# New job orders for a two-layer decoder kernel, and its four weight-folding jobs moved five periods ahead

## The reference

```python
x = x + _L0_attn_ref(_layernorm(x), ...)    # 16 heads of 16, softmax
x = x + _L0_xattn_ref(_layernorm(x), ctx)   # 16 heads, 120 context rows, softmax
x = x + _L0_ffn_ref(_layernorm(x), ...)     # 256x256 weight quantised to int4, plus rank 16
x = x + _L1_attn_ref(_layernorm(x), ...)    # rotary positions, sigmoid instead of softmax
x = x + _L1_xattn_ref(_layernorm(x), ctx)   # one head of 256, softmax
x = x + _L1_ffn_ref(_layernorm(x), ...)     # two of 64 experts per 128 tokens
```

## Time and profile before

| | us |
|---|---|
| median of 3 runs (lowest, highest) | 1092.66 (1091.53, 1095.04) |
| the profiled execution | 1096.01 |
| its span | 1094.2 |
| PE busy in it | 1020.1 (93%) |
| DVE busy | 762.7 (70%) |
| ACT busy | 635.6 (58%) |
| POOL busy | 583.9 (53%) |

### The profile page before, as it was taken

The page is one execution under the profiler, slowest core; times in us unless marked ns, Lnnn a source line. Parts: engine busy times, 40 slices in busy tenths (PEclk is TensorE's granted clock), DMA queues, the critical chain, the costliest instruction groups (busy, mean ns, idle before and its releaser), DMA issues.

```text
span 1094.2 us, 24132 instructions
## 1 busy us (share of the span) xinstructions
PE 1020.1 (93%) x8386; PEld 799.5 (73%) x8386; DVE 762.7 (70%) x1736; ACT 635.6 (58%) x1150; POOL 583.9 (53%) x924
## 2 busy tenths in 40 slices
...
GB/s 205 89 102 82 120 99 79 123 62 79 92 82 68 51 84 80 97 118 93 93 81 81 41 79 73 89 83 81 84 74 91 85 105 64 15 76 166 186 181 197
DMA packets 123484, 104.81 MB, mean 96 GB/s; under 512 B 26826, under 2 KB 123099, under 8 KB 123355
## 3 DMA queue, kind: packets, MB, share of 16 engines
...
## 4 chain that ended last, share of the span: by engine, by line
PE 83%; DVE 9%; issue 3%; DMA 2%; ACT 2%; POOL 1%; ACTq 0%; DVEq 0%; SPq 0%; POOLq 0%
PE l_ring L1217 11%; PE l_sT L1132 11%; PE l_o L1152 11%; PE l_copy L1198 9%; PE l_ring L1254 7%; PE l_ring L1167 7%; PE l_ring L1237 4%; PE l_copy L1175 4%; PE l_ring L1874 3%; DVE l_nmax L984 3%; PE l_copy L1152 3%; PE l_ring L1265 2%; PE l_sT L1813 2%; PE l_copy L1245 1%; PE l_o L1846 1%
## 5 line engine op out<-in xcount | busy, mean ns | idle before, releaser
L984 DVE TENSOR_REDUCE l_nmax<-l_ring 128x2 f32<-128x512 f32 (+1 forms) x384 | 250.7, 676 | 104.2 <-PE l_ring L1167 101.4
L763 ACT ACTIVATE l_probs<-l_sT 128x1024 f32<-128x1024 f32 (+1 forms) x256 | 257.8, 1025 | 58.9 <-PE l_sT L1132 45.9
L1132 PE MATMUL l_sT<-qstack,kstack 99*128 99x256 bf16 (+2 forms) x1280 | 187.4, 273 | 0.9 <-ACT l_probs L763 0.5
L1167 PE MATMUL l_ring<-kstack,qstack 96*128 96x256 bf16 (+1 forms) x1024 | 141.5, 247 | 26.7 <-issue 16.3
L1132 PEld LDWEIGHTS l_sT<-qstack,kstack 99*128 99x128 bf16 (+2 forms) x1280 | 125.8, 104 | 25.1 <-issue 2.7
L1167 PEld LDWEIGHTS l_ring<-kstack,qstack 96*128 96x128 bf16 x1024 | 78.1, 98 | 79.2 <-issue 32.0
L1217 PE MATMUL l_ring<-wT,l_zT 128*128 128x256 f32 x512 | 126.8, 386 | 1.7 <-DVE l_attn L1022 0.7
L1152 PE MATMUL l_o<-l_probs,v_heads 128*32 128x256 f32 (+1 forms) x2048 | 127.8, 384 | 0.0
L1198 PE MATMUL l_copy<-l_zT,wT 128*128 128x256 f32 x384 | 104.0, 404 | 4.8 <-ACT l_zT L808 2.8
L1217 PEld LDWEIGHTS l_ring<-wT,l_zT 128*128 128x128 f32 x512 | 92.5, 192 | 14.6 <-issue 2.6
L616 POOL TENSOR_SCALAR factors<-mv 128x2 f32<-128x2 f32 (+1 forms) x77 | 19.4, 253 | 155.8 <-DVE mv L1041 86.4
...
## 6 DMA issues: line engine op xcount, KB each, us to landing
...
```

The lines of the kernel that those rows point to most:

```text
L763: act.activation(probs[buffer_of(g)][0:kp, :], sT[g % 2][0:kp, :], ACT.Sigmoid if sig(u) else ACT.Exp, scale=HD ** -0.5).then_inc(p_ok, 1)
L984: dve.tensor_reduce(nmax[u % 2][:, tt, h0:h0 + hb], bank("s", u, i)[:, 0:hb * sk].rearrange("p (h k) -> p h k", h=hb), AX_X, ALU.max, nega ...
L1132: i = pe.matmul(sT[g % 2][0:kp, j * S:(j + 1) * S], kstack[slot_of(u)][0:rows_used, col * width(u) + kt * kp:col * width(u) + (kt + 1) * k ...
L1167: m = pe.matmul(out[:, j * sk:(j + 1) * sk], qstack[slot_of(u)][0:STACK, (h0 + j) * S + tt * P:(h0 + j) * S + (tt + 1) * P], kstack[slot_o ...
```

## The change

Only the tables change, and one lookup. `jobs_of` now asks for a list of the period's own before it takes that of the kind:

```diff
-    for word in ORDERS[kind].split():
+    for word in ORDERS.get(f"p{p}", ORDERS[kind]).split():
```

Periods 1, 12 to 16, 28 to 38, 44 and 45 get such lists (those of 12 to 15 equal the new `self` list). The list of `cross` stays; that of `sigmoid` only loses the four fold words. `FILL`, `FIRST_PERIOD`, `DRAIN`, `TAIL_ORDER` and `END` have the same jobs as before in a new order, and the fold jobs have other periods:

```diff
 ORDERS = {
     "self": """
-        np qa sT0 dq0 s sT1 p0q s qb s s pv2 e0 o1 pv3 e1 p0k s s dq1 ka s kb p1q e2 e3 p2q oT1 sT2 sT3 p1k dk1 dk0 dq2
-        q0 dk2 s va rows vb l2 s lf lo nT qm pv0 p2k o0 pv1 xb s q1 aT s sT4 e4 l1 s s z e5 oT0 sT5 s qA sT6 cl xs w s
-        pa e6 lw xf cx st pb sT7 ws e7 fac s qB""",
+        sT0 p0q qa dq0 s sT1 s qb np s s pv2 e0 pv3 o1 e1 s s ka s kb p0k dk0 p1q oT1 sT2 e2 dq1 p2q dq2 sT3 e3 nT p1k
+        dk1 s p2k dk2 lo l1 l2 va q0 rows vb s pv0 pv1 o0 s aT s s sT4 e4 s z cl e5 oT0 ws qm q1 sT5 s qA sT6 e6 fac xs
+        xb s w pa cx e7 st xf pb s lw lf sT7 qB""",
...
 FILL = (
-    "xs:0 wi dq0:0 xs:1 rows:0 z:0 xf:0 bi xf:1 bv rows:1 qa:0 qb:0 ka:0 p0q:0 p0k:0 kb:0 p1q:0 p1k:0 p2q:0 dq1:0 "
-    "z:1 dk1:0 ka:1 kb:1 dk0:0 qa:1 dk2:0 qb:1 dq2:0 p1q:1 dk0:1 z:2 p2k:0 p1k:1 va:0 dq1:1 dq0:1 p0q:1 p0k:1 xs:2 "
...
+    "xf:0 wi xs:0 rows:0 bi xs:1 z:0 xf:1 qa:0 qb:0 bv p0q:0 ka:0 kb:0 dq0:0 p0k:0 dk0:0 dk1:0 rows:1 z:1 p1q:0 "
+    "dq1:0 p1k:0 dk2:0 qa:1 qb:1 p2q:0 dq2:0 p2k:0 dq0:1 p0q:1 ka:1 kb:1 p1q:1 dq1:1 z:2 xs:2 dk0:1 p0k:1 p1k:1 "
...
-        "qB": (15,), "t.w": (20,), "ma": (35,), "mb": (36,), "mc": (37,), "md": (38,)}
+        "qB": (15,), "t.w": (20,), "ma": (30,), "mb": (31,), "mc": (32,), "md": (33,)}
...
-TAIL_ORDER = "add s q cl hash choose rows2 y pT z v fac rows out mean cx z2"
+TAIL_ORDER = "cl s q hash fac choose rows2 y pT z rows v out cx z2 add mean"
```

More of the change, by code:

```diff
@@ new lines @@
+    "p12": """
+        sT0 p0q qa dq0 s sT1 s qb np s s pv2 e0 pv3 o1 e1 s s ka s kb p0k dk0 p1q oT1 sT2 e2 dq1 p2q dq2 sT3 e3 nT p1k
+        dk1 s p2k dk2 lo l1 l2 va q0 rows vb s pv0 pv1 o0 s aT s s sT4 e4 s z cl e5 oT0 ws qm q1 sT5 s qA sT6 e6 fac xs
+        xb s w pa cx e7 st xf pb s lw lf sT7 qB""",
+    "p13": """
+        sT0 p0q qa dq0 s sT1 s qb np s s pv2 e0 pv3 o1 e1 s s ka s kb p0k dk0 p1q oT1 sT2 e2 dq1 p2q dq2 sT3 e3 nT p1k
+        dk1 s p2k dk2 lo l1 l2 va q0 rows vb s pv0 pv1 o0 s aT s s sT4 e4 s z cl e5 oT0 ws qm q1 sT5 s qA sT6 e6 fac xs
+        xb s w pa cx e7 st xf pb s lw lf sT7 qB""",
@@ new lines @@
+    "p14": """
+        sT0 p0q qa dq0 s sT1 s qb np s s pv2 e0 pv3 o1 e1 s s ka s kb p0k dk0 p1q oT1 sT2 e2 dq1 p2q dq2 sT3 e3 nT p1k
+        dk1 s p2k dk2 lo l1 l2 va q0 rows vb s pv0 pv1 o0 s aT s s sT4 e4 s z cl e5 oT0 ws qm q1 sT5 s qA sT6 e6 fac xs
+        xb s w pa cx e7 st xf pb s lw lf sT7 qB""",
+    "p15": """
+        sT0 p0q qa dq0 s sT1 s qb np s s pv2 e0 pv3 o1 e1 s s ka s kb p0k dk0 p1q oT1 sT2 e2 dq1 p2q dq2 sT3 e3 nT p1k
+        dk1 s p2k dk2 lo l1 l2 va q0 rows vb s pv0 pv1 o0 s aT s s sT4 e4 s z cl e5 oT0 ws qm q1 sT5 s qA sT6 e6 fac xs
+        xb s w pa cx e7 st xf pb s lw lf sT7 qB""",
@@ new lines @@
+    "p16": """
+        qa sT0 qb s t.w pv2 pv3 e0 p0q sT1 s np p0k ka e1 o1 s kb s rope_k p2k p1q sT2 dq0 oT1 nT p1k fr dk0 va sT3 aT
+        vb s rope_q s dq1 dk1 ffac fst pv0 o0 p2q dq2 fb rows pv1 xb s cx pa e2 pb fxb fac fz z st kT dk2 cl fa qT oT0
+        s e3""",
+    "p28": """
+        sT0 qa np qb s e0 pv2 t.w p0q pv3 o1 p0k s s sT1 e1 ka kb s oT1 sT2 nT va dq0 dk0 dq1 e2 dq2 fxb vb dk2 rope_k
+        fr s sT3 aT p1k cx s pv0 pv1 p2k s p2q rows cl p1q pa o0 e3 fz pb st xb rope_q fa fb oT0 fst z kT dk1 fac qT s
+        ffac""",
@@ new lines @@
+    "p29": """
+        t.w sT0 e0 ka p1q np kb qa qb s p0q rope_q o1 dq0 pv2 pv3 s sT1 s nT s sT2 oT1 fr p2k va vb dq1 e1 pv0 aT o0
+        rope_k dk2 p0k dk0 s sT3 dq2 e2 s pv1 p2q dk1 fz cl fxb cx rows s e3 st pa fst pb qT p1k fac fa fb z oT0 xb
+        ffac s kT""",
+    "p30": """
+        s p0k sT0 dq1 e0 e1 qa p0q qb np o1 sT1 pv2 pv3 t.w ka p1q p2q s s p1k kb oT1 s dk2 s nT rope_q sT2 ma fr s sT3
+        e2 va s aT rope_k pv0 p2k pv1 fxb vb cl dq2 dk1 dq0 fz xb dk0 rows s pa qT fst fac st o0 e3 pb z fa fb oT0 cx
+        kT ffac""",
@@ new lines @@
+    "p31": """
+        sT0 sT1 t.w qa np e0 p1k p0k p0q s qb pv2 pv3 dq1 o1 e1 ka s kb p2k s s oT1 rope_q sT2 sT3 va e2 fr mb vb p1q s
+        st rope_k aT dq0 p2q nT s cx pv0 pv1 dk2 fxb ffac dq2 dk1 o0 pa rows xb fz pb qT fa fac e3 fb z s fst cl oT0 kT
+        s dk0""",
+    "p32": """
+        o1 dk0 p0q pv2 pv3 e0 rope_q qa qb oT0 pv0 fr sT0 e1 p1q o0 rope_k e2 sT1 dq2 ka p0k kb pv1 oT1 sT2 mc st rows
+        xb sT3 va e3 dk2 dq0 aT vb p1k p2q fz e4 sT4 dk1 sT5 fst pa z e5 pb sT6 p2k qT fac e6 fa fxb dq1 sT7 fb kT ffac
+        e7""",
@@ new lines @@
+    "p33": """
+        p0q p1q qa dk0 qb dk1 pv0 dq0 pv1 rope_q fr o0 o1 dq2 e0 rope_k pv2 pv3 oT0 fxb sT0 sT1 oT1 ka sT2 p0k e1 aT kb
+        rows xb dq1 e2 sT3 md st va dk2 fz e3 e4 p2q vb fst sT4 pa z pb sT5 fa e5 sT6 qT p2k p1k fb fac sT7 e6 e7 ffac
+        kT""",
+    "p34": """
+        qa o0 rope_q o1 qb pv0 dq0 dq2 fr dk1 pv1 pv2 rope_k p0q pv3 p1q oT0 sT0 e0 oT1 e1 sT1 p0k ka dk0 e2 kb fxb dk2
+        aT rows e3 sT2 va sT3 st vb fz sT4 p1k e4 pa p2k z sT5 fst p2q e5 pb fac ffac dq1 fa kT sT6 sT7 fb xb qT e6 e7""",
```

33 lines of the change are left out of this document (28 added, 5 removed), and 28 rows, old and new, of tables (DRAIN, FILL, FIRST_PERIOD).

## The result

The changed kernel takes 1074.91 us (median of 4, 1074.1 to 1078.05), the kernel before 1092.78 beside it (4 runs, 1091.53 to 1095.04): ratio 0.984, 95% interval 0.9814 to 0.9865. Forecast were 1071 us, range 1061 to 1081: the time lies inside, 3.9 us above the forecast. The profiled execution took 1074.1 us, its span 1072.2.

What follows compares the result with a forecast made beforehand. PE was taken as the bound, busy 1020.1 of 1094.2 us, with order able to close only part of its missing 74.1. Savings summed to 21.5 us; from the median 1092.66 this gave 1071 us, 8-in-10 range 1061 to 1081.

Steps and rivals of the forecast that it cites:

- Period 12: Unit 14's last key part goes ahead of POOL's reduction, so PE's 8.20 us gap closes; saving 8.5 us, bounds 3.0 and 9.7.
- Self periods: Key copies issued earlier shorten PE's waits before a unit's first score maximum; saving 4 us, bounds 1 and 5.
- Filling and period 0: Start of the kernel: new order closes PE's waits while three units are prepared; saving 5 us, bounds 0 and 9.
- Fold jobs, own lists: Folded-weight jobs leave periods 35 to 38 for 30 to 33, saving 1 us; own lists at the passages, saving 1.
- `DRAIN`, `TAIL_ORDER`: Periods 47 to 60: PE's order unchanged, additions on POOL go behind the factors; saving 0.5 us, bounds -1 and +1.
- The end: Last stretch: the second `hash` comes earlier, as `z2` of 15 no longer waits for `y` of 10; saving 1.5 us.
- the sign: Whole kernel: the prediction is wrong if PE's idle time falls by much less than 18 us in total.
- the early reading: Period 12: POOL's hold begins when it reaches the reduction, so `np` is ready at 335.3 and `nT` waits 1.4 us.
- the far end: Period 12's lower bound: 5.2 us of waiting and the clock falling again for 2.9, saving only 3.0 us.
- The rival of the transfers: Filling: PE's work closes up but stacks land when they did; that term goes to 0, 1076.2 us; chance 0.10.
- the slower rival: Periods 28 to 38, 44 and 45: own lists open new waits, 2.2 us a period, 28.6 in all; 1099.8 us; chance 0.06.

Runs made afterwards that it cites:

- e1: The kernel before with one edit: in period 11 the last part of unit 14's keys goes ahead of the largest weight and its reduction; 1087.78 us, ratio 0.9952.
- e2: The changed kernel with biases, largest weight and its reduction again ahead of unit 14's last part, in period 11 alone; 1082.11 us, ratio 0.9907.
- e9: The changed kernel with the largest weight found by two transfers and a DVE maximum instead of POOL's reduction; 1070.65 us, ratio 0.9787.
- e3: The changed kernel with the lists for the filling and period 0 of the kernel before; 1080.34 us, ratio 0.989.
- e7: The changed kernel with POOL's last four additions left out, signals kept; 1073.05 us, ratio 0.9817.
- e11: The changed kernel without own lists for periods 28 to 38, 44 and 45, folded-weight jobs at their old places; 1078.64 us, ratio 0.9851.
- e5: The changed kernel with POOL's four last additions moved: two ahead of the factors of sequence 14, two right behind them; 1074.1 us, ratio 0.982.
- e12: The changed kernel with one more reduction over partitions on POOL at its start, result unused; 1081.81 us in one run.
- e6: The changed kernel with the last list (END) of the kernel before, TAIL_ORDER staying new; 1074.22 us, ratio 0.9817.

## Why the prediction held, term by term

Measured is the mean of the stretches with the old list less the mean with the new one, over all traces that have it.

| Term | Forecast | Measured |
|---|---|---|
| Period 12 (12 to 15) | 8.5 (3.0 to 9.7) | 8.1 |
| Self periods (1 to 11) | 4 (1 to 5) | 2.7 |
| Filling and period 0 | 5 (0 to 9) | 5.6 |
| Fold jobs, own lists | 1 + 1 | 1.8 + 1.2 = 3.0 |
| `DRAIN`, `TAIL_ORDER` (46 to 59) | 0.5 | 0.5 |
| Periods 16 to 27 | 0 | 0.4 |
| The end | 1.5 (0 to 4) | -1.5 |
| Sum | 21.5 | 18.8 |

The times differ by 17.9 us. The two profiled executions alone differ by 21.95, within half a microsecond of the forecast sum: that agreement is luck. The one of before lay 3.2 us above its median, mostly by its filling, the one of after 0.8 below. The terms fall 2.7 us short of the forecast: the end by 3.0 and the self periods by 1.3, against 1.6 more from all others together. So the time lies inside the range partly because errors cancelled. PE's idle time fell by 15.0 us, less than the 18 that I had named as the sign, and its busy time by 7.0, as less of it ran at half clock.

*Period 12* was right in cause (e1, e2) and size (11.1 - 2.5 is 8.6, not the 8.5 that I wrote). `np` was forecast at 335.3, 10.5 us after the start of period 12, and PE's arrival at `nT` 9.1 after it; they were 10.9 and 9.2 (325.3 and 323.57), and the wait of 1.81 is near the 1.4 of the early reading. Missed was the wait of unit 15's first maximum (0.78), behind the same hold; e9, without the hold, has neither. A small wait is not always cheap: in e3, e7 and e11 `nT` waited 1.8 to 2.0 us too, PE's clock fell behind it (mean 0.94 from 315 to 345 in e7, 1.00 in the changed kernel's trace), and period 12 took 24.3 to 24.6 instead of 22.8. I had priced the fall only at the far end. The length of the wait doesn't decide it: in e5 `nT` waited 2.3 us at 1.00. The GPSIMD Engine Reference of the Trainium skill (Instruction dispatch) has about 6 us at the first call. By this the traces agree in size in period 11 (5.4 to 5.7), not in count: e12 shows the hold at the second call as well. Nor does the wait come on top of the hold: the 5.63 us have 2.6 us of waiting for the maximum inside. That the code is exchanged each time is the natural reading; the rows show only the holds.

*Self periods*, right in sign, 1.3 too large: I had the copies go 2 us earlier and most of the waits gone. A unit's last copy is issued 1.1 us earlier (16.7 to 15.6 us into its period, mean of ten) and lands 0.4 earlier, since copies take longer (the page's median for the 128 KB key copies went from 4.4 to 5.3 us, and the DMA share of the stretch from 0.59 to 0.67). So 2.7 of the 4.5 us of waiting stayed, where I had written under 1.5. DVE's largest weight, moved, also held a bank that `pa` of unit 10 waited 0.77 for.

*Filling*, right: the third `z` at 36.4 (forecast 35 to 39). The first came no later at all (16.98 in both traces; forecast 1.3 later): PE was done with the weights 1.0 us sooner, at 13.1, and then waited 1.0 longer. The rival of the transfers was wrong, though they are busier (0.90).

*Fold jobs and lists*: 35 to 38 fell to the length of their neighbours as forecast; 30 to 33 grew by 0.8 us, less than the 1 to 3 forecast. No wait of note stands in the sigmoid periods; the slower rival's place is empty.

*The end* failed, in two steps, and cost 1.5 us where 1.5 were to be gained. The first said that "the chain to `z2` of sequence 14 (4.87 idle) goes through the same DVE jobs as before". It does, but they got longer: I moved POOL's additions in the order without asking what runs beside them. From the first `hash` to this `z2` it took 5.0 to 5.1 us with the old list (before, e1, e6), 6.2 to 6.6 with the new one, and 3.1 without the additions (e7). The trace of before had the sign, a small DVE operation of 1.2 us beside one addition, and I did not look for it. The SBUF page of the Trainium skill (SBUF: two separate sides) says that such a pair shares a port as an exclusive lock, for a DVE operation with two SBUF inputs or in a mode that takes two ports. The three operations of 1.0 us beside additions of 1.26, and 0.15 to 0.21 without them (e7), agree.

The second step was the gain itself: `z2` of 15 ahead of `y` of 10. I put its start 0.7 us, and the second `hash` 6.4 us, after the start of `z2` of 14. They came 2.4 and 8.5 us after it: the two `z2` write the same bank, and PE stood 1.32 us until ACT had emptied it (the row at 1042.59), a wait for which the sum had no term. The old list has 7.6 to 8.6 us for this piece, the new one 8.0 to 8.5, and e7, without the additions, 8.5. So this step gained nothing that the traces show.
